# A decoder kernel's first attention: one power for two norms, a second transposed tile, no loop, and the causal mask added by VectorE

## The chip, the cores and the metric

The kernel runs on one core of a Trainium2 chip. The metric is the device time of one execution in microseconds. A core has TensorE (PE), VectorE (DVE), ScalarE (ACT), GpSimd (POOL) and SyncE (SP, which issues the DMAs here). Each works through its own queue in order; semaphores order them against one another. PSUM has 8 banks; one holds 512 float32 per partition.

## The reference

A two-layer decoder on x of 16 batches x 128 tokens x 256 features. The change lies in layer 0's self attention, which in short is:

```
h  = layernorm(x)                      # plain; it is added back below
hn = layernorm(h) * ln_g + ln_b        # a second norm on the first
q, k, v = hn @ wq.T + bq, hn @ wk.T + bk, hn @ wv.T + bv   # 16 heads x 128
q, k = rope(q), rope(k)
p  = softmax(q @ k.T / sqrt(128) + causal)                 # per head, 128 x 128
x  = x + h + (p @ v) @ wo.T + bo
```

This is the first 590 us of the kernel. Retention, a spline layer, window attention, cross attention and a mixture of experts follow, and the change leaves their work as it is.

## The kernel before, in words

`phase_attn0` takes four batches at a time (a group, NG = 4 groups) and in each group one head per step (16 steps), 64 steps in all. Every product that matters is made of three (`matmul3`): operands are kept as a rounded high part and a low rest, in float32r. `step(s, r, g)` is written for each engine: s is the step, r the head, g the group. Step s projects q, k and (in r 0 to 13) one or two pieces of v for head s, works the softmax of head s-2 and the output product of head s-3. `run` writes group 0 out, loops over groups 1 and 2 with a hardware loop (`Fori`), and writes group 3 and three draining steps out.

The order on each engine in a step:

- PE (L604): `project(s)`, with `project_v` behind q and k; a `transpose_x` of the next group's batch in r 5, 7, 9, 11; `out_project(s-3)`; `transpose_p(s-2)`; `score(s-1)`, which first multiplies the bf16 mask with a bf16 identity into the bank SC (L589) and then adds q k^T on top (L592); `weigh(s-2)` (L601).
- DVE (L475): the row maximum of SC for s-2 (L479), `oT_lo` (L482), the reciprocal and P times it (L488), `rope` of q and k (two products each, L455 and L456), then what the step has besides: in group 0 the split of a weight item (L411, r 0 to 12), `add_h` (which adds the norm h to X, L442 and L444), statistics. In r 3, `add_out` (L464) stands before the ropes and `add_const` (L469, L473) behind them.
- ACT (L357): four exponentials with row sums (L363), `sin_q`, a V evacuation, `sin_k` (L372, L380), PT (L386), oT_hi (L390), in group 0 the rounding of weight items.
- POOL: the addition of the two rope products (L322), and the powers to -1/2 (L316, L334).

The high and low parts of the transposed input lie in one pair of tiles, `xT_hi` and `xT_lo`. The next group's are made in r 15: ACT rounds (L355), DVE splits (L448) between the rope of q and the rope of k, and the projection of the next group's head 0 waits for that.

Weights come through two staging buffers (`stage`), in the order of `ITEMS`; an item is loaded, rounded by ACT and split by DVE. The retention phase's inputs are later loaded into the same memory.

Before the first step: statistics of group 0, a power for the first norm, three small DVE operations, a second power, then for each batch in turn normalise (L437), transpose (L539) and evacuate (L348), through one buffer and one bank.

## Time and profile before

| | us |
|---|---|
| median of three runs | 1178.92 (1178.39 to 1179.3) |
| the profiled execution | 1178.37 |
| its span, first to last instruction | 1176.3 |

| engine | busy us | share of the span |
|---|---|---|
| PE | 1023.7 | 87% |
| DVE | 793.6 | 67% |
| ACT | 715.3 | 61% |
| POOL | 315.8 | 27% |

The shares are means over phases with different limits. Starts are counted from the first instruction. A matmul's end is modelled and lies behind the start of the next, so that TensorE is best read by the distance between starts. "idle before <- X" tells how long an engine had stood still and whose result it then had.

### The profile page before, as it was taken

What the parts mean: (1) busy time and instruction counts of PE and PEld (TensorE: products, weight loads), DVE (VectorE), ACT (ScalarE), POOL (GpSimd) and SP (SyncE); (2) the same over time, 40 slices, a digit from 0 to 9 for tenths busy, and PEclk for the clock granted to TensorE, in tenths of its full rate; (3) what the DMA queues carried; (4) which work ended last, traced back from release to release, by engine and by line L of the source; (5) the groups of instructions that cost most, each with busy time, mean ns of one, the idle gap of its engine ahead of it and who ended that gap; (6) DMA issues with size and microseconds to landing.
All of it is one profiled execution on the core that took longest, in us unless ns stands there. A gap on an engine that the chain in (4) does not pass through costs nothing. (4 is left out here: it accounts for less than half of the span.)

```text
span 1176.3 us, 19320 instructions
## 1 busy us (share of the span) xinstructions
PE 1023.7 (87%) x6729; PEld 841.8 (72%) x6757; DVE 793.6 (67%) x1461; ACT 715.3 (61%) x1974; POOL 315.8 (27%) x244
## 2 busy tenths in 40 slices
PE   2789899999899999999878867289999599598997
PEld 2677788888788988898777656267776499474555
DVE  3888876777677766766656777767777534365774
ACT  3577776677667776667533364177777244456883
POOL 1343332323223332232300020134444200101442
PEclk9999999999999999999989878599999799799999
DMA  6111110000000000000070000000000000005342
GB/s 180 55 54 54 37 32 1 1 1 1 2 1 1 1 1 1 1 1 1 1 202 1 1 1 1 1 1 1 2 1 2 1 1 1 14 1 140 102 108 72
DMA packets 31978, 31.80 MB, mean 27 GB/s; under 512 B 8336, under 2 KB 23440, under 8 KB 31888
## 3 DMA queue, kind: packets, MB, share of 16 engines
q1 hardware_dynamic: 31888, 30.60, 9.3%
q8 instruction: 57, 0.93, 0.3%
q14 instruction: 33, 0.27, 0.1%
HBM read 28.36 MB, written 2.23 MB: 26 GB/s over the span
## 5 line engine op out<-in xcount | busy, mean ns | idle before, releaser
L322 POOL TENSOR_TENSOR roped_q<-roped_q,sin_q 128x512 f32<-128x512 f32 x64 | 81.9, 1279 | 323.5 <-DVE sin_q L456 323.5
L35 PE MATMUL banks<-xT_lo,WH 128*128 128x512 f32 x256 | 107.4, 420 | 8.4 <-issue 5.9
L1501 ACT ACTIVATE win_P<-banks,win_neg_max 128x128 f32<-128x128 f32 x256 | 91.1, 382 | 31.2 <-DVE win_neg_max L1567 30.9
L322 POOL TENSOR_TENSOR roped_k<-roped_k,sin_k 128x512 f32<-128x512 f32 x64 | 95.8, 1497 | 52.3 <-DVE sin_k L456 52.3
L363 ACT ACTIVATE P<-banks,neg_max 128x128 f32<-128x128 f32 x256 | 90.3, 370 | 30.8 <-DVE neg_max L479 30.8
L36 PE MATMUL banks<-xT_hi,WL 128*128 128x512 f32 x256 | 102.0, 398 | 0.0
L37 PE MATMUL banks<-xT_hi,WH 128*128 128x512 f32 x256 | 101.9, 398 | 0.0
L390 ACT ACTIVATE oT_hi<-banks,bv_col 128x512 fp32r<-128x512 f32 x64 | 44.1, 688 | 87.6 <-PE banks L601 87.6
L1460 POOL TENSOR_TENSOR win_P<-win_P,win_inv 128x512 f32<-128x512 f32 x64 | 66.6, 1040 | 100.5 <-DVE win_inv L1572 100.3
L372 ACT ACTIVATE sin_k<-banks 64x512 f32<-64x512 f32 x128 | 75.8, 592 | 10.1 <-PE banks L37 8.5
L372 ACT ACTIVATE sin_q<-banks 64x512 f32<-64x512 f32 x128 | 75.8, 592 | 7.7 <-PE banks L37 5.5
L601 PE MATMUL banks<-PT,V 128*128 128x128 f32 x512 | 70.0, 280 | 11.8 <-ACT PT L386 11.8
L582 PE MATMUL banks<-WO_lo,oT_hi 128*128 128x256 f32 x256 | 74.6, 291 | 4.7 <-DVE oT_lo L482 4.7
L601 PEld LDWEIGHTS banks<-PT,V 128*128 128x128 f32 x512 | 62.8, 193 | 15.4 <-ACT PT L386 15.4
L582 PE MATMUL banks<-WO_hi,oT_lo 128*128 128x256 f32 x256 | 72.6, 284 | 0.0
L582 PE MATMUL banks<-WO_hi,oT_hi 128*128 128x256 f32 x256 | 72.3, 282 | 0.0
L592 PEld LDWEIGHTS banks<-roped_k,roped_q 128*128 128x128 f32 x512 | 68.1, 194 | 2.4
L455 DVE SCALAR_TENSOR_TENSOR roped_k<-banks,qk_bias,cos 128x512 f32<-128x512 f32 x64 | 48.0, 750 | 30.9 <-ACT sin_k L372 30.9
L592 PE MATMUL banks<-roped_k,roped_q 128*128 128x128 f32 x512 | 68.3, 277 | 0.0
L2123 POOL TENSOR_TENSOR moe_acc<-moe_acc,moe_weighted 128x512 f32<-128x512 f32 x30 | 38.6, 1289 | 105.6 <-DVE moe_weighted L2241 105.6
L482 DVE SCALAR_TENSOR_TENSOR oT_lo<-banks,bv_col,oT_hi 128x512 fp32r<-128x512 f32 x64 | 47.7, 746 | 28.5 <-ACT oT_hi L390 27.9
L455 DVE SCALAR_TENSOR_TENSOR roped_q<-banks,qk_bias,cos 128x512 f32<-128x512 f32 x64 | 48.0, 750 | 23.9 <-ACT sin_q L372 23.9
(359 smaller groups left out, 3045.1 us busy)
## 6 DMA issues: line engine op xcount, KB each, us to landing
moe_gate_of<-moe_gate_rows SPq DMA_DIRECT2D x32, 256.0 KB, 4.0
X<-in_x SPq DMA_DIRECT2D x4, 512.0 KB, 7.0
stage<-in_wqT SPq DMA_DIRECT2D x4, 512.0 KB, 3.8
stage<-in_wkT SPq DMA_DIRECT2D x4, 512.0 KB, 3.7
stage<-in_wvT SPq DMA_DIRECT2D x4, 512.0 KB, 6.4
stage<-in_woT SPq DMA_DIRECT2D x4, 512.0 KB, 3.8
ctx<-in_ctxT SPq DMA_DIRECT2D x4, 512.0 KB, 6.5
out<-X SPq DMA_DIRECT2D x8, 256.0 KB, 2.8
```

The lines of the kernel that those rows point to most:

```text
L35: nc.tensor.matmul(out, lh, rl, start=first, stop=False)
L36: nc.tensor.matmul(out, ll, rh, start=False, stop=False)
L37: return nc.tensor.matmul(out, lh, rh, start=False, stop=last)
L322: nc.gpsimd.tensor_tensor(roped[w][:, p, :], roped[w][:, p, :], sin_part[w][:], ALU.add).then_inc(roped_sum[w], 1)
L363: ins = nc.scalar.activation(P[:, i, :], SC[:, i * 128:(i + 1) * 128], ACT.Exp, bias=neg_max[:, r % 2, i:i + 1], accum_out=exp_sum[:, r % ...
L372: ins = nc.scalar.activation(sin_part[w][64 * half:64 * half + 64, :], QK[w][64 * (1 - half):64 * (2 - half), :], ACT.Copy)
L455: nc.vector.scalar_tensor_tensor(per_batch(roped[w][:, p, :]), per_batch(QK[w][:]), qk_bias[:, w, r:r + 1], table(cos), ALU.add, ALU.mult) ...
L582: ins = nc.tensor.matmul(OUT[i // 2][:, i % 2 * D:(i % 2 + 1) * D], lhs[:, i, :], rhs[:, ur, :], start=False, stop=True, skip_group_check= ...
L592: ins = nc.tensor.matmul(SC[:, i * 128:(i + 1) * 128], roped[0][:, p, toks], roped[1][:, p, toks], start=False, stop=True, skip_group_chec ...
L601: ins = nc.tensor.matmul(PO[:, i * 128:(i + 1) * 128], V[:, ur // 4 % 2, i, h * 128:(h + 1) * 128], PT[:, i, :], start=True, stop=True)
L1460: nc.gpsimd.tensor_tensor(some, some, inv[:, h % 2, 4 * s:4 * s + 4].rearrange("p (h n) -> p h n", n=1).broadcast_to([128, 4, 128]), ALU.m ...
L1501: ins = nc.scalar.activation(P[:, h % 2, s, i, :], SC[2 * (h % 2) + s][:, i * 128:(i + 1) * 128], ACT.Exp, bias=neg_max[:, h % 2, at:at + ...
```

## The change

1. **One power.** DVE works out the variance of both norms together: with v the variance, `var12 = v * (1 + eps) + eps^2` ahead of one power gives the factor of both (`rstd12`); a second power gives the first norm's own (`rstd`), which only `add_h` needs. `second_norm` and its operations go.
2. **The start.** The first group's four batches are normalised into V's second half, transposed into two banks, and evacuated by two activations; rounding and splitting go by halves. A third staging buffer (over P and PT) holds the third weight item; the order of the first items becomes q, v, k; a projection waits only for its own item.
3. **A tile for odd groups.** `xT_of` is `xT_even` (whose memory the retention inputs take later, as `ret_in`) and `xT_odd` (over the staging buffers). The next group's halves are made in r 13 (ACT) and at the end of r 14 (DVE).
4. **No loop.** All 67 steps are written out, on POOL too.
5. **The mask.** The float32 mask stays as it is loaded. DVE adds it to SC in place, then takes the maximum; the bf16 product, `ident_b` and the bf16 mask go.
6. **Moves.** `add_h` of a group's four batches goes to r 12 to 15 of that group (before: r 0 to 3 for group 0, and r 5, 7, 9, 11 of the group ahead for the others). `add_out` goes from before the ropes of r 3 to the end of r 2. In group 0 the other groups' statistics go from r 0 to 2 to r 4 to 6, the norms to r 7, the normalises to r 8 to 11. The final statistics of groups 0 to 2 go from r 12 to r 8 of group 3.

```diff
-stage = sb("stage", [128, 2, KD, QW])
+with ExitStack() as first:
+    xT_even = sb("xT_even", [128, 2, KD, QW], F32R, first)
+ret_in = sb("ret_in", [128, 2, KD, QW])
...
 cos = sb("cos", [128, 2, S])
 sin = sb("sin", [128, 2, S])
-mask_f = h_of[:, 0:128]
 zeros_b = sb("zeros_b", [128, 128], BF16)
 gb = sb("gb", [128, 2, KD])
 bv_col = sb("bv_col", [128, HEADS0])
-xT_lo = sb("xT_lo", [128, KD, GW], F32R)
+with ExitStack() as first:
+    stage = sb_("stage", [128, STAGES, KD, QW], F32, first)
 sin_part = [sb("sin_q", [128, GW]), sb("sin_k", [128, GW])]
 V = sb("V", [128, 2, GROUP, QW])
+with ExitStack() as first:
...
-ITEMS = [(0, 0), (0, 1), (0, 2)] + [item for q in range(1, QUADS) for item in ((q, 2), (q - 1, 3), (q, 0), (q, 1))] + [(QUADS - 1, 3)]
+ITEMS = [(0, 0), (0, 2), (0, 1)] + [item for q in range(1, QUADS) for item in ((q, 2), (q - 1, 3), (q, 0), (q, 1))] + [(QUADS - 1, 3)]
+def staging(i):
+    if i == STAGES:
+        return stage_P[:], stage_loaded[STAGES], 16
...
-LN_PARTS = ((slice(0, GROUP), GROUP), (slice(GROUP, B), B + 11))
+LN_PARTS = ((slice(0, GROUP), GROUP), (slice(GROUP, B), B + 8))
...
 def run(eng, step):
-        step((NG - 1) * HEADS0 + r, r, NG - 1)
-    for r in range(3):
-        step(STEPS + r, r, NG)
+    for s in range(STEPS + 3):
+        step(s, s % HEADS0, s // HEADS0)
+prepared_at = lambda g: (8, 9, 10, 11) if g == 0 else (4, 6, 8, 10)
+PREPARED = 13
 with nc.Block() as block:
...
-            wait(sp, weights_split, i - STAGES + 1)
+            if i > STAGES:
+                sp.wait_ge(weights_split, i - STAGES if i < 5 else i - 1)
             if w == 3:
                 src = woT[:, 4 * q:4 * q + 4, :]
             else:
                 src = w_src[w][:, :, q * QW:(q + 1) * QW]
-            sp.dma_start(parts(i)[0], src).then_inc(stage_loaded[i % STAGES], 16)
...
-        for i in range(STAGES):
+        for i in range(STAGES + 1):
             load_weights(i)
-        for dst, src in ((mask_f, a["causal"]),
...
-        sp.wait_ge(weights_split, len(ITEMS))
-        held = stage[:].rearrange("p s k n -> p (s k n)")
+        sp.wait_ge(projected[1], (NG - 1) * HEADS0)
+        sp.wait_ge(v_projected, (NG - 1) * HEADS0)
...
+        def powers(part):
             some, n = LN_PARTS[part]
-            pool.wait_ge(ln0, n + 7 + 3 * second)
-            nc.gpsimd.tensor_tensor((rstd, rstd2)[second][:, some], var_eps[:, some], minus_half[:, some], ALU.pow).then_inc(rstd_ready, 1)
+            pool.wait_ge(ln0, n + 8)
+            nc.gpsimd.tensor_tensor(rstd12[:, some], var12[:, some], minus_half[:, some], ALU.pow).then_inc(rstd_ready, 1)
+            nc.gpsimd.tensor_tensor(rstd[:, some], var_eps[:, some], minus_half[:, some], ALU.pow).then_inc(rstd_ready, 1)
         def step(t, p):
...
+        for t in range(STEPS):
             step(t, t % 2)
-            if t in (2, 3):
-                power(1, t - 2)
-        with pool.Fori(2, STEPS // 2) as i:
-            for p in range(2):
-                step(i * 2 + p, p)
-        pool.wait_ge(ln0, B + 29)
+            if t == 7:
+                powers(1)
...
+            wait(act, xT_split, KD * group)
             for k in range(KD):
             ins.then_inc(xT_evacuated, 1)
+        def first_xT():
+            act.wait_ge(x_transposed, GROUP)
+            for k in range(KD):
+                nc.scalar.activation(xT_full[:, k, :], bank[3 + k], ACT.Identity, bias=gb[:, 1, k:k + 1], scale=gb[:, 0, k:k + 1]).then_inc(xT_evacuated, GROUP // KD)
+            for k in range(KD):
+                act.wait_ge(xT_evacuated, GROUP // KD * (k + 1))
+                nc.scalar.activation(xT_even[:, 0, k, :], xT_full[:, k, :], ACT.Copy).then_inc(xT_rounded, 1)
         def round_xT(g):
             act.wait_ge(xT_evacuated, GROUP * g + GROUP)
-            wait(act, projected[1], HEADS0 * g)
-            nc.scalar.activation(xT_hi[:], xT_full[:], ACT.Copy).then_inc(xT_rounded, 1)
+            if g == 1:
+                act.wait_ge(weights_split, len(ITEMS))
+            wait(act, projected[1], HEADS0 * (g - 1))
...
                 act.wait_ge(max_found, 1 + u)
+                if u == 0:
+                    act.wait_ge(weights_split, STAGES + 1)
...
-            if r == 15 and live(g + 1, NG):
+            if r == PREPARED and g + 1 < NG:
                 round_xT(g + 1)
...
-        for i in range(STAGES):
-            round_weights(i)
+            if g + 1 < NG and r - 1 in prepared_at(g):
+                i = prepared_at(g).index(r - 1)
+                evacuate_xT((g + 1) * GROUP + i, i, g + 1)
+        round_weights(0)
         act.wait_ge(first_loaded, 48)
-        for b in range(GROUP):
-            evacuate_xT(b, b, 0)
-        round_xT(0)
+        first_xT()
+        round_weights(1)
         round_weights(2)
...
+            nc.vector.tensor_scalar(var12[:, some], ln_tmp[:, 4, some], (1.0 + LN_EPS) / D, LN_EPS * LN_EPS, ALU.mult, ALU.add).then_inc(ln0, 1)
...
-            wait(dve, x_transposed, b)
-            nc.vector.tensor_scalar(xn[:], batch(X, b), one(mean, b), one(rstd12, b), ALU.subtract, ALU.mult).then_inc(xn_ready, 1)
+            dve.wait_ge(rstd_ready, 1 if b < GROUP else 3)
+            if b >= GROUP:
+                dve.wait_ge(x_transposed, b)
+            dst = V[:, 1, b, 0:D] if b < GROUP else xn[:]
+            nc.vector.tensor_scalar(dst, batch(X, b), one(mean, b), one(rstd12, b), ALU.subtract, ALU.mult).then_inc(xn_ready, 1)
...
+            dve.wait_ge(rstd_ready, 2 if b < GROUP else 4)
...
-            dve.wait_ge(xT_rounded, g + 1)
-            nc.vector.tensor_tensor(xT_lo[:], xT_full[:], xT_hi[:].bitcast(F32), ALU.subtract).then_inc(xT_split, 1)
+            for k in (range(KD) if g == 0 else (slice(0, KD),)):
+                dve.wait_ge(xT_rounded, k + 1 if g == 0 else KD * g + KD)
+                nc.vector.tensor_tensor(xT_of[g % 2][:, 1, k], xT_full[:, k], xT_of[g % 2][:, 0, k].bitcast(F32), ALU.subtract).then_inc(xT_split, 1 if g == 0 else KD)
...
                 dve.wait_ge(scored, u + 1)
+                nc.vector.tensor_tensor(SC.rearrange("p (h n) -> p h n", h=GROUP), SC.rearrange("p (h n) -> p h n", h=GROUP), four(mask[:]), ALU.add).then_inc(masked, 1)
+                dve.wait_ge(masked, u + 1)
                 nc.vector.tensor_reduce(neg_max[:, r % 2, :], SC[:].rearrange("p (h n) -> p h n", h=GROUP), AX.X, ALU.max, negate=True).then_inc(max_found, 1)
...
-                if r == 3 and live(g - 1, NG):
-                    add_out(g - 1)
                 rope(s, r % 2, r, 0)
-                if r == 15 and live(g + 1, NG):
-                    split_xT(g + 1)
                 rope(s, r % 2, r, 1)
-            if isinstance(g, int) and g == 0:
+            if g == 0:
                 for i in split_at(r):
                     split_weights(i)
-                if r < GROUP:
-                    add_h(r)
-                if r < 3:
-                    group_stats(r + 1)
-                if r in (2, 3, 4):
-                    (first_stats, second_stats, both_norms)[r - 2](1)
-            if r == 3 and live(g - 1, NG):
+                if r in (4, 5, 6):
+                    group_stats(r - 3)
+                if r == 7:
+                    both_norms(1)
+            if r == 2 and 0 < g < NG:
+                add_out(g - 1)
+            if r == 3 and 0 < g < NG:
                 add_const(g - 1)
-            if r == 12 and isinstance(g, int) and g == NG - 1:
+            if r == 8 and g == NG - 1:
                 dve.wait_ge(restated, NEXT)
-                finish_stats(nc, dve, ln0, B + 22, stats[:, 0:NEXT, :], mean[:, 0:NEXT], var_eps[:, 0:NEXT], ln_tmp[:, :, 0:NEXT], LN_EPS)
-            if r in (4, 6, 8, 10) and live(g + 1, NG):
-                normalise(g * GROUP + GROUP + (r - 4) // 2)
-            if r in (5, 7, 9, 11) and live(g + 1, NG):
-                add_h(g * GROUP + GROUP + (r - 5) // 2)
+                finish_stats(nc, dve, ln0, B + 16, stats[:, 0:NEXT, :], mean[:, 0:NEXT], var_eps[:, 0:NEXT], ln_tmp[:, :, 0:NEXT], LN_EPS)
+            if g + 1 < NG and r in prepared_at(g):
+                normalise((g + 1) * GROUP + prepared_at(g).index(r))
+            if g + 1 < NG and r == PREPARED + 1:
+                split_xT(g + 1)
+            if g < NG and r >= HEADS0 - GROUP:
+                add_h(g * GROUP + r - (HEADS0 - GROUP))
...
-        first_stats(0)
-        split_weights(0)
-        second_stats(0)
-        split_weights(1)
         both_norms(0)
+        dve.wait_ge(ln0, GROUP + 8)
         for b in range(GROUP):
             normalise(b)
+        split_weights(0)
+        split_xT(0)
+        split_weights(1)
+        split_weights(2)
         dve.wait_ge(consts_loaded, 16 * 11)
-        nc.vector.tensor_copy(ident_b[:], ident[:]).then_inc(consts_made, 1)
-        nc.vector.tensor_copy(mask[:], mask_f).then_inc(consts_made, 1)
         nc.vector.memset(zeros_b[:], 0.0).then_inc(consts_made, 1)
-        split_xT(0)
-        split_weights(2)
...
-            wait(pe, xT_evacuated, b)
+            if b >= GROUP:
+                pe.wait_ge(xT_evacuated, b)
             for k in range(KD):
-                ins = nc.tensor.transpose(XB[:, k * 128:(k + 1) * 128], xn[:, k * 128:(k + 1) * 128], ident[:])
+                dst, src = (bank[3 + k][:, b * S:(b + 1) * S], V[:, 1, b, :]) if b < GROUP else (XB[:, k * 128:(k + 1) * 128], xn)
+                ins = nc.tensor.transpose(dst, src[:, k * 128:(k + 1) * 128], ident[:])
...
-                pe.wait_ge(xT_split, g + 1)
-            if isinstance(g, int) and g == 0 and r % 4 == 0:
-                pe.wait_ge(weights_split, split_by[r // 4, 1])
+                pe.wait_ge(xT_split, KD * (g + 1))
             cols = slice(r * DK0, (r + 1) * DK0)
+            xT_hi, xT_lo = xT_of[g % 2][:, 0], xT_of[g % 2][:, 1]
             for w in range(2):
+                if g == 0 and r % 4 == 0:
+                    pe.wait_ge(weights_split, split_by[r // 4, w])
...
-            nc.tensor.matmul(SC[:], ident_b[:], four(mask[:]), start=True, stop=True)
+            if u == 0:
+                pe.wait_ge(consts_made, 1)
             for i in range(GROUP):
                 toks = slice(i * S, (i + 1) * S)
-                ins = nc.tensor.matmul(SC[:, i * 128:(i + 1) * 128], roped[0][:, p, toks], roped[1][:, p, toks], start=False, stop=True, skip_group_check=True)
+                ins = nc.tensor.matmul(SC[:, i * 128:(i + 1) * 128], roped[0][:, p, toks], roped[1][:, p, toks], start=True, stop=True)
...
-            if r in (5, 7, 9, 11) and live(g + 1, NG):
-                transpose_x(g * GROUP + GROUP + (r - 5) // 2)
+            if g + 1 < NG and r - 1 in prepared_at(g):
+                transpose_x((g + 1) * GROUP + prepared_at(g).index(r - 1))
```

## Rows read from the trace of the kernel before

**Rows 1.** Windows: stretch, length, busy us and instructions per engine, granted clock, DMA share, GB/s.

```profile
170.00:310.00 140.00, 134.92 (x839) 118.81 (x840) 100.70 (x156) 96.54 (x258) 43.41 (x33) 0.99 0.00 1
```

**Rows 2.** Timeline, TensorE: start, duration, engine, line, operation. Scores of steps 17, 28, 33, 44, 49, 60.

```profile
189.61 1.05 PE L592 MATMUL banks<-roped_k,roped_q 128*128 128x128 f32 x8
...
281.27 1.05 PE L592 MATMUL banks<-roped_k,roped_q 128*128 128x128 f32 x8
...
326.58 1.05 PE L592 MATMUL banks<-roped_k,roped_q 128*128 128x128 f32 x8
...
418.25 1.05 PE L592 MATMUL banks<-roped_k,roped_q 128*128 128x128 f32 x8
...
460.61 1.05 PE L592 MATMUL banks<-roped_k,roped_q 128*128 128x128 f32 x8
...
551.28 1.05 PE L592 MATMUL banks<-roped_k,roped_q 128*128 128x128 f32 x8
```

**Rows 3.** Timeline, VectorE: the maximum in steps 2, 7, 8, 9, 13, 14, 16, 63, 64.

```profile
44.44 0.68 DVE L479 TENSOR_REDUCE neg_max<-banks 128x4 f32<-128x512 f32 x1
...
94.89 0.68 DVE L479 TENSOR_REDUCE neg_max<-banks 128x4 f32<-128x512 f32 x1
...
104.48 0.68 DVE L479 TENSOR_REDUCE neg_max<-banks 128x4 f32<-128x512 f32 x1
...
113.62 0.68 DVE L479 TENSOR_REDUCE neg_max<-banks 128x4 f32<-128x512 f32 x1
...
149.79 0.68 DVE L479 TENSOR_REDUCE neg_max<-banks 128x4 f32<-128x512 f32 x1
...
156.50 0.68 DVE L479 TENSOR_REDUCE neg_max<-banks 128x4 f32<-128x512 f32 x1
...
172.30 0.68 DVE L479 TENSOR_REDUCE neg_max<-banks 128x4 f32<-128x512 f32 x1
...
567.89 0.68 DVE L479 TENSOR_REDUCE neg_max<-banks 128x4 f32<-128x512 f32 x1
...
574.60 0.68 DVE L479 TENSOR_REDUCE neg_max<-banks 128x4 f32<-128x512 f32 x1
```

**Rows 4.** Timeline, VectorE: sin product of k in step 63, beside GpSimd's addition.

```profile
573.35 1.32 DVE L456 SCALAR_TENSOR_TENSOR sin_k<-sin_k,rot_bias,sin 128x512 f32<-128x512 f32 x1
```

**Rows 5.** Timeline, VectorE and GpSimd: second half of an add_h, and the addition beside it.

```profile
225.21 1.38 DVE L444 TENSOR_TENSOR X<-X,h_of 128x256 f32 x1
...
224.92 1.37 POOL L322 TENSOR_TENSOR roped_k<-roped_k,sin_k 128x512 f32<-128x512 f32 x1 [0.78 <-DVE sin_k L456]
```

**Rows 6.** Timeline: mask product and scores of a step, its maximum, the first exponential.

```profile
526.91 0.38 PE L589 MATMUL banks<-mask,ident_b 128*128 128x512 bf16 x1
...
527.13 1.05 PE L592 MATMUL banks<-roped_k,roped_q 128*128 128x128 f32 x8
...
528.22 0.69 DVE L479 TENSOR_REDUCE neg_max<-banks 128x4 f32<-128x512 f32 x1 [0.32 <-PE banks L592]
...
529.70 0.36 ACT L363 ACTIVATE P<-banks,neg_max 128x128 f32<-128x128 f32 x1
```

**Rows 7.** Groups by line, to 590 us: shapes, count, busy us, mean ns, idle before.

```profile
L464 DVE TENSOR_TENSOR X<-banks,X 128x512 f32 x4 | 2.6, 683 | 0.0
...
L455 DVE SCALAR_TENSOR_TENSOR roped_k<-banks,qk_bias,cos 128x512 f32<-128x512 f32 x64 | 48.0, 750 | 30.9 <-ACT sin_k L372 30.9
```

**Rows 8.** Timeline: first power, first normalise, first projection product.

```profile
7.38 1.02 POOL L316 TENSOR_TENSOR rstd<-var_eps,minus_half 128x4 f32<-128x4 f32 x1 [6.54 <-DVE var_eps L61]
...
13.97 0.41 DVE L437 TENSOR_SCALAR xn<-X,mean,rstd 128x256 f32<-128x256 f32 x1
...
23.49 0.77 PE L35 MATMUL banks<-xT_lo,WH 128*128 128x512 f32 x1 [3.29 <-issue]
```

**Rows 9.** Windows: 3 us behind TensorE's wait at the loop's second pass; its first product.

```profile
307.50:310.50 3.00, 2.64 (x6) 2.15 (x7) 1.12 (x3) 1.21 (x8) 0.34 (x1) 0.52 0.02 5
...
307.86 0.79 PE L35 MATMUL banks<-xT_lo,WH 128*128 128x512 f32 x1 [2.56 <-issue]
```

More of the change, by code:

```diff
@@ L182, in phase_attn0 @@
         consts_loaded = sem("consts_loaded")
-        stage_loaded = [sem(f"stage{i}_loaded") for i in range(STAGES)]
+        stage_loaded = [sem(f"stage{i}_loaded") for i in range(STAGES + 1)]
         weights_rounded = sem("weights_rounded")
@@ L345, in evacuate_xT @@
                     act.wait_ge(x_transposed, b + 1)
-                    wait(act, xT_split, group)
+                    wait(act, xT_split, KD * group)
                     for k in range(KD):
@@ L2430, in weights_ahead, with phase_rest @@
     return w, transfers
-def phase_rest(nc, a, sem, sb, banks, bank, X, ident, mean, var_eps, rstd, minus_half, stats, ln_tmp, out, clear_semaphores, free_attn0, stage, out_bias, ret_loaded):
+def phase_rest(nc, a, sem, sb, banks, bank, X, ident, mean, var_eps, rstd, minus_half, stats, ln_tmp, out, clear_semaphores, free_attn0, ret_in, out_bias, ret_loaded):
     t = (nc, a, sem, sb, bank, X, ident, mean, var_eps, rstd, minus_half, stats, ln_tmp)
```

65 lines of the change are left out of this document (26 added, 39 removed).

## The prediction

> **What bounds the kernel now.** First I read busy time by stretch. Between 170 and 310 us TensorE is busy 96% of the time, VectorE 72%, ScalarE 69%, the granted clock at 0.99 [rows 1]. So the first attention (to about 590 us) is mostly TensorE's, and everything behind 590 us is untouched by the diff. Then I read when the scores of successive steps begin (one step is one head of one group of four batches; I count steps 0 to 63, and by "score n" I mean the start of step n's score products) and when VectorE's maximum begins [rows 2, 3]. Score 49 to score 60 takes 90.67 us for eleven steps, mostly 8.05 each. But in group 0 the maxima are 9.59 and 9.14 apart, and there TensorE waits.
>
> A second circle turns there, which I call the **round**: maximum (0.6), four exponentials (1.5), sin_q (1.2), V (0.6) and sin_k (1.2) in order on ScalarE, k's rope on VectorE (1.4), VectorE's extra work of the step, then the next maximum. Bare, it takes 6.71 (149.79 to 156.50). In a step without V it takes 6.71 as well (567.89 to 574.60): V's evacuation falls away, but the sin product of k then runs beside GpSimd and takes 1.32 [rows 3, 4]. In group 0 the weight split with a normalise makes 9.14, with an add_h 9.59. An add_h alone, beside GpSimd's addition of 1.37, holds VectorE 1.74 us (its second half alone is 1.38) [rows 5]. Whatever makes a round longer than TensorE's step of 8.05 (6.65 without V) sets the pace as soon as the slack of some 2 us is used.
>
> **The change, part by part.**
>
> *The mask.* TensorE loses the bf16 product: 526.91 to the score at 527.13 is 0.22 us in each of 64 steps [rows 6]. VectorE gains a 128x512 add in place in PSUM. No row shows VectorE writing PSUM. The nearest is the add of a bank and X, 0.683; the rope product that reads a bank and a table takes 0.750 [rows 7]. I bound it by 0.55 and 0.85 (with its wait) and take 0.69 and 0.04 for the handoff to the maximum, 0.73 in all, as it is nearest to the first. Where TensorE paces, the add is covered: today the maximum starts at 528.22, 1.09 after the score at 527.13, but ScalarE comes to the exponentials only at 529.70, 2.57 after it, because oT_hi is in front of them [rows 6]; mask and maximum end at 1.09 + 0.73 + 0.65 = 2.47. There the step gains 0.22. Where the round paces, the step loses 0.73. A covered add would thus be worth 14 us of TensorE time over 64 steps, an uncovered one costs 47.
>
> The rope product with one operand in a bank keeps 0.75 with GpSimd running, that with both in SBUF takes 1.32 [rows 4, 7]. The Trainium skill (GPSIMD Engine Reference, 1. Specifications) says VectorE and GpSimd collide when VectorE has two SBUF inputs or uses a 2-port mode; by it the mask add, with one SBUF input, isn't lengthened but add_h is, and the trace agrees. The same skill (VectorE: DVE Perf Modes, Rules for kernel authors) tells authors to minimise the number of chained operations, semaphores being free; that speaks against a second pass over the scores. By its table (The TRN2 errata) a 512-element pass with a PSUM source is 120 + 512 cycles at 0.96 GHz, 0.66 us, an estimate by which the total would be 1 us lower.
>
> *The start.* Today the first projection begins at 23.49 [rows 8]. Afterwards one power instead of two stands before the normalise. GpSimd starts the first at 7.38 and takes 1.02; the second follows at once and holds off the first normalise until about 9.4. Four normalises (0.41 each, the last part of one under the start of the next) end at 10.8 [rows 8]. The four batches go to two banks without waiting for one another, so the transposes are in at 11.5. ScalarE then takes two 128x512 evacuations and two roundings of 0.6 (to 13.9), VectorE two splits of 0.65, the second behind the last rounding (to 14.7). First projection 14.9: **-8.6**. The third weight's transfer now stands before the constants in the queue; it is 512 KB and is needed only at about 17, the constants too.
>
> *Projection to first maximum.* Today 44.44 - 23.49 = 20.95 [rows 3, 8]. VectorE's two add_h (1.8 each) and two sets of statistics (1.3 each) leave the queue ahead of it, 6.2; a little of that was covered by waits: **-5.6**.
>
> *Group 0, first maximum to that of step 13.* Today 149.79 - 44.44 = 105.35 [rows 3]. All of it is rounds, so all pay 0.73. Steps 2 and 3 (split only): 7.84 + 0.73 = 8.57 each; steps 4 to 6 with statistics 9.9 each; step 7 with the small ones of the norms 10.0; steps 8 to 11 9.14 + 0.73 = 9.87 each; step 12 with split and add_h 9.59 + 0.73 = 10.32. Sum 106.65: **+1.3**. The two powers between steps 7 and 8 hold GpSimd 4.6 us, done before the next rope.
>
> *Group 0, steps 13 to 16.* Rounds: 13: 6.71 + 0.73 + 1.74 = 9.18; 14, with the split of xT and add_h: 6.71 + 0.73 + 2.88 = 10.32; 15: 9.18. Sum 28.7 against 172.30 - 149.79 = 22.51 [rows 3]: **+6.2**. From there to score 17, 17.31 today [rows 2, 3], the mask comes once, the product goes: **+0.3**.
>
> *Middles.* Score 17 to 28 is 91.66 today, 49 to 60 90.67 [rows 2]. Eleven times 0.22 is -2.4; constants and statistics stay at step 3, where the mask makes a late round later still: +1.2. **-1.2** in groups 1 and 2, **-0.3** in group 3, where the final statistics move to step 8. Moving add_out ahead of step 3 relieves TensorE of 0.3; counted in.
>
> *Boundaries.* Score 28 to 33 is 45.31, score 44 to 49 42.36 [rows 2]. The difference, 2.95, is the loop's branch: TensorE is idle 2.56 us before 307.86, and the granted clock falls to 0.52 over the next 3 us, which is the lower level, 1.2 GHz [rows 9]. Afterwards nothing branches, and the double xT lets projections go on. But all four add_h now stand in steps 12 to 15, two of which have no V and need TensorE only 6.43. In rounds from score 27: mask 1.45 behind it, step 12 9.6 (ScalarE evacuates xT before the exponentials), then 9.18, 10.32, 9.18, and 17.4 to score 33: 57.1, less 7.8 to score 28: 49.3. **+4.0** and **+6.9**. Before, each add_h of these groups stood in a step with 8.05 us of TensorE's work and was hidden.
>
> *End.* Group 3 had no add_h; now it has four. From score 60 to the maximum of step 64 it was 574.60 - 551.28 = 23.32 [rows 2, 3]; now 2.6 + 3 x 9.18 = 30.1, **+6.8**, and **+0.3** in the tail, where the mask is partly beside oT_hi.
>
> Sum: -8.6 - 5.6 + 1.3 + 6.2 + 0.3 - 1.2 - 1.2 - 0.3 + 4.0 + 6.9 + 7.1 = +8.9. At each boundary TensorE will wait 2 to 3 us at once, which as at the branch can halve the clock for its next products [rows 9]. Three times about 0.5, mostly inside waits: +1.5. The profiled execution took 1178.37 us around a span of 1176.3, 0.55 below the median of 1178.92. 1178.37 + 10.4 = 1188.8; against the median 1189.
>
> **The rivals.**
> *TensorE stays the bound* (the faster side). If slack between the queues takes up the late add_h, boundaries fall to TensorE's own work: 0 instead of +6.2, -4.1 and -1.1 instead of +4.0 and +6.9, -0.7 at the end. Sum -21: 1158. For it speaks TensorE's 96% [rows 1]; against it group 0, where rounds of 9.59 pace steps worth 8.05 [rows 3]. It decides at a round of 6.43 + 2 in step 14; I forecast 10.3. 12%.
> *add_h is short* when it misses GpSimd: 0.75 instead of 1.74, 16 times with 1 us each but partly slack: about 1176. For it: the first halves are 0.4. Against: GpSimd starts its addition 0.13 behind the product each time [rows 5]. 8%.
> *The start gains nothing*, the change not doing what it says, as the third weight or the constants land late: +5 at most, 1194. 8%.
> *The mask in PSUM is dear*, 0.85 or more, or each stall also halves the clock: some 30 round-paced steps at 0.12 and more, and 1.7 per drop: 1196 to 1204. 12%.
> *The forecast* 60%, 1182 to 1195, by the mask's two bounds.
>
> **How the numbers follow.** The range 1174 to 1200 leaves out the first rival and the dearest part of the fourth, about 17%. A measurement can tell about 0.2%, 2.4 us, from no change. Faster: both first rivals, 0.20. Same: the edges between, 0.06. Slower 0.74.
>
> **What the profile would show.** First projection near 15 us; the mask add at 0.69 and maxima 0.73 behind it; score to score 7.83 in group 3's middle; 10.3 between maxima of steps 14 and 15, with TensorE waiting for P and PT there; score 44 to 49 near 49; the end of the first attention about 10 us later than 587. I am wrong if TensorE shows no waits in steps 13 to 16, or if add_h takes under 1 us.

## The result: 1.3% slower, and where the time went

The changed kernel takes 1194.04 us (median of 4, 1193.29 to 1197.06), the kernel before 1178.66 (1177.82 to 1179.3): a ratio of 1.0134, 95% interval 1.0115 to 1.0152. The profiled execution took 1193.29 us around a span of 1191.5, so the two traces are 15.2 us apart in span. Among the executions of the experiments below two took far longer, one of the kernel before (1877 us) and one with the mask product back (3451 us), and the ratios leave them out. The forecast was 1189, slower, with a range of 1174 to 1200.

From the page of the kernel after (busy us, share and instructions):

```profile
PE 1020.9 (86%) x6665; PEld 836.6 (70%) x6693; DVE 836.6 (70%) x1518; ACT 717.5 (60%) x1969; POOL 318.6 (27%) x244
```

VectorE has 43 us more to do than before (793.6), TensorE 3 less (1023.7). That alone doesn't say what is lost. The scores of steps 17, 28, 33, 44, 49 and 60 after, in the timeline of TensorE (start, duration, engine, line, operation), answer to [rows 2]:

```profile
184.59 1.06 PE L602 MATMUL banks<-roped_k,roped_q 128*128 128x128 f32 x8
...
275.52 1.06 PE L602 MATMUL banks<-roped_k,roped_q 128*128 128x128 f32 x8
...
326.52 1.06 PE L602 MATMUL banks<-roped_k,roped_q 128*128 128x128 f32 x8
...
416.74 1.06 PE L602 MATMUL banks<-roped_k,roped_q 128*128 128x128 f32 x8
...
466.31 1.06 PE L602 MATMUL banks<-roped_k,roped_q 128*128 128x128 f32 x8
...
557.19 1.06 PE L602 MATMUL banks<-roped_k,roped_q 128*128 128x128 f32 x8
```

At score 17 the changed kernel is 5.02 us ahead (189.61 before); it loses that and more at the two boundaries and at the end. By the stages of the forecast, in us, changes of length:

| stage | before | after | change | forecast |
|---|---|---|---|---|
| to the first projection | 23.49 | 14.63 | -8.9 | -8.6 |
| to the first maximum | 20.95 | 17.06 | -3.9 | -5.6 |
| group 0, to the maximum of step 13 | 105.35 | 107.34 | +2.0 | +1.3 |
| to the maximum of step 16 | 22.51 | 28.72 | +6.2 | +6.2 |
| to score 17 | 17.31 | 16.84 | -0.5 | +0.3 |
| middle, scores 17 to 28 | 91.66 | 90.93 | -0.7 | -1.2 |
| boundary, 28 to 33 | 45.31 | 51.00 | +5.7 | +4.0 |
| middle, 33 to 44 | 91.67 | 90.22 | -1.4 | -1.2 |
| boundary, 44 to 49 | 42.36 | 49.57 | +7.2 | +6.9 |
| middle, 49 to 60 | 90.67 | 90.88 | +0.2 | -0.3 |
| score 60 to the end of the attention | 36.30 | 44.96 | +8.7 | +7.1 |
| everything behind it | 588.72 | 589.35 | +0.6 | 0 |

The last row is work that the change leaves alone. In the kernels below it lies between 588.1 and 592.5, with the places where the clock is lowered, so that a single trace of a span says nothing under some 4 us; the stages in front of it repeat much more closely (below, two kernels agree in them within 0.04).

What such a stretch looks like in the changed kernel, here in group 0, steps 14 and 15: VectorE's timeline (same columns; split of xT, add_h, mask, maximum; then add_h, mask, maximum), with ScalarE's first exponential between the two. In brackets stands the idle time ahead of an instruction, and whose result it then had:

```profile
154.94 1.21 DVE L458 TENSOR_TENSOR xT_odd<-xT_full,xT_odd 128x1024 fp32r<-128x1024 f32 x1
156.07 1.38 DVE L451 TENSOR_SCALAR h_of<-X,mean,rstd 128x256 f32<-128x256 f32 x1
157.48 0.42 DVE L453 TENSOR_TENSOR X<-X,h_of 128x256 f32<-128x256 f32 x1
157.82 0.69 DVE L489 TENSOR_TENSOR banks<-banks,mask 128x512 f32<-128x512 f32 x1
158.55 0.69 DVE L491 TENSOR_REDUCE neg_max<-banks 128x4 f32<-128x512 f32 x1
...
159.28 0.37 ACT L379 ACTIVATE P<-banks,neg_max 128x128 f32<-128x128 f32 x1 [3.38 <-DVE neg_max L491]
...
165.27 0.40 DVE L451 TENSOR_SCALAR h_of<-X,mean,rstd 128x256 f32<-128x256 f32 x1
165.70 1.40 DVE L453 TENSOR_TENSOR X<-X,h_of 128x256 f32<-128x256 f32 x1
167.03 0.69 DVE L489 TENSOR_TENSOR banks<-banks,mask 128x512 f32<-128x512 f32 x1
167.75 0.69 DVE L491 TENSOR_REDUCE neg_max<-banks 128x4 f32<-128x512 f32 x1
```

On VectorE split, add_h, mask and maximum follow one another with no idle time, and ScalarE waits for the maximum, 3.38 us here. Between the two maxima lie 9.20 us (the forecast had 9.18), in the step before, with the split, 10.34 (10.32); before, the round of step 13 took 6.71 [rows 3].

And TensorE waits for it. From its timeline at the first boundary:

```profile
300.36 0.39 PE L591 MATMUL banks<-WO_lo,oT_hi 128*128 128x256 f32 x1 [2.43 <-DVE oT_lo L494]
...
304.30 1.16 PE L611 MATMUL banks<-PT,V 128*128 128x128 f32 x8 [0.57 <-ACT PT L402]
...
312.27 0.50 PE L35 MATMUL banks<-WL,xT_even 128*128 128x512 f32 x1 [2.71 <-ACT V L396]
...
313.61 0.63 PE L37 MATMUL banks<-WH,xT_even 128*128 128x512 f32 x1
...
317.16 1.06 PE L602 MATMUL banks<-roped_k,roped_q 128*128 128x128 f32 x8
```

V's evacuation (L396) frees the bank that the second product of V for head 0 needs; it stands behind sin_q in ScalarE's queue, so behind the late maximum of 308.14. TensorE had run ahead into the next group and stood still there for 2.71 us. Some 1.1 us later its clock is halved (the row of 313.61: 0.63 where such a product takes 0.39). The same two places at the second boundary:

```profile
453.58 0.50 PE L35 MATMUL banks<-WL,xT_odd 128*128 128x512 f32 x1 [2.02 <-ACT V L396]
...
456.93 1.06 PE L602 MATMUL banks<-roped_k,roped_q 128*128 128x128 f32 x8
```

The wait for V is there as well, and it ends at the same place: 36.75 us behind score 28 at the first boundary, 36.84 behind score 44 at the second. The next score comes at 41.64 and at 40.19. So the 1.4 us by which the first boundary is the longer lie behind the wait, where the first has the lowered clock and the second 1.00. The window with the lowered clock (length; busy us and instructions of PE, PEld, DVE, ACT, POOL; granted clock, DMA share, GB/s):

```profile
313.40:316.80 3.40, 3.40 (x16) 3.20 (x15) 1.47 (x2) 0.64 (x2) 2.28 (x2) 0.50 0.00 0
```

0.50 is the lower level, 1.2 GHz, for 3.4 us in which TensorE is busy throughout, on the path to score 32.

### The profile page after: what moved, and what is told of

Its sections match the earlier page's. It is cut to its first block and busy times, and to the rows that moved or that the text cites. A ratio compares the mean times of both kernels' runs of the same rounds, so it can differ in the third digit from the quotient of the medians.

```text
span 1191.5 us, 18922 instructions
## 1 busy us (share of the span) xinstructions
PE 1020.9 (86%) x6665; PEld 836.6 (70%) x6693; DVE 836.6 (70%) x1518; ACT 717.5 (60%) x1969; POOL 318.6 (27%) x244
## 5 line engine op out<-in xcount | busy, mean ns | idle before, releaser
L329 POOL TENSOR_TENSOR roped_k<-roped_k,sin_k 128x512 f32<-128x512 f32 x64 | 99.5, 1555 | 43.8 <-DVE sin_k L466 43.8
L611 PE MATMUL banks<-PT,V 128*128 128x128 f32 x512 | 73.4, 287 | 26.3 <-ACT PT L402 26.1
L591 PEld LDWEIGHTS banks<-WO_lo,oT_hi 128*128 128x128 f32 x256 | 49.1, 192 | 29.0 <-DVE oT_lo L494 23.8
L602 PEld LDWEIGHTS banks<-roped_k,roped_q 128*128 128x128 f32 x512 | 63.5, 195 | 0.1
L2236 DVE TENSOR_TENSOR moe_hidden<-banks,moe_squared 128x512 f32<-128x512 f32 x64 | 44.1, 689 | 27.0 <-PE banks L2343 18.0
L1576 DVE TENSOR_REDUCE win_neg_max<-banks 128x8 f32<-128x1024 f32 x32 | 39.2, 1224 | 28.2 <-PE banks L1705 28.2
L35 PE MATMUL banks<-xT_even,WH 128*128 128x512 f32 x128 | 53.8, 420 | 3.5 <-DVE xT_even L458 3.5
```

Of the source, the lines that this page charges most:

```text
L35: nc.tensor.matmul(out, lh, rl, start=first, stop=False)
L329: nc.gpsimd.tensor_tensor(roped[w][:, p, :], roped[w][:, p, :], sin_part[w][:], ALU.add).then_inc(roped_sum[w], 1)
L591: ins = nc.tensor.matmul(OUT[i // 2][:, i % 2 * D:(i % 2 + 1) * D], lhs[:, i, :], rhs[:, ur, :], start=False, stop=True, skip_group_check= ...
L602: ins = nc.tensor.matmul(SC[:, i * 128:(i + 1) * 128], roped[0][:, p, toks], roped[1][:, p, toks], start=True, stop=True)
L611: ins = nc.tensor.matmul(PO[:, i * 128:(i + 1) * 128], V[:, ur // 4 % 2, i, h * 128:(h + 1) * 128], PT[:, i, :], start=True, stop=True)
L2236: TT(dst, U1[s % 3], squared[:, s % 2, :], ALU.mult).then_inc(hidden_done, 1)
```

## The experiments

The theory to be tested: what counts is the round (maximum, exponentials, sin_q, V, sin_k, k's rope, VectorE's extras). The mask costs each round-paced step 0.73, and add_h costs 1.8 in each because it stands where no wait covers it. The rivals: TensorE's own slack, the clock, or the written-out loop are behind the loss.

### add_h back in the middle: where it hurts depends on the mask

For groups 1 to 3, `add_h` goes from r 12 to 15 to r 5, 7, 9, 11 of its own group.

```diff
-if g < NG and r >= HEADS0 - GROUP:
+if g == 0 and r >= HEADS0 - GROUP:
     add_h(g * GROUP + r - (HEADS0 - GROUP))
+if 0 < g < NG and r in (5, 7, 9, 11):
+    add_h(g * GROUP + (r - 5) // 2)
```

> The changed kernel with the add_h of groups 1 to 3 moved from steps 12 to 15 of a group to its steps 5, 7, 9 and 11; group 0 and all else as changed. Theory of the round (mask 0.73 and add_h 1.74 both lengthen the circle through VectorE and ScalarE): a middle step with add_h now has a round of 7.44 + 1.74 = 9.18 against TensorE's 7.88, so what the boundaries give back is mostly lost in the middles: about 1191 us, 3 less than changed. Rival (the place at the boundary is the cause, since two of those steps have no V): the boundaries of groups 1 to 2, 2 to 3 and the end lose their +5.7, +7.2 and +8.7 us and nothing comes in their place: about 1173 us.

Measured: 1188.26 us, ratio to before 1.0074 (1.0046 to 1.0101), span 1185.9. Scores 28 to 33 now take 44.11, 44 to 49 44.27, the end 39.77: 6.9, 5.3 and 5.2 less. But the middles take 93.83, 93.60 and 94.58: 2.9, 3.4 and 3.7 more. In the kernel before the same place was free: there, with an add_h or a normalise of the same steps in front of it, the maximum begins 1.5 to 2.2 behind the scores, and ScalarE comes to the exponentials 2.6 to 3.3 behind them anyway, because oT_hi and in some steps an evacuation of xT are in front. Here, with the mask add as well, the maximum begins 3.6 to 3.7 behind the scores, and ScalarE waits for it. Scores, mask, maximum and first exponential of one step of this run:

```profile
219.70 1.06 PE L604 MATMUL banks<-roped_k,roped_q 128*128 128x128 f32 x8
...
222.69 0.69 DVE L489 TENSOR_TENSOR banks<-banks,mask 128x512 f32<-128x512 f32 x1
...
223.41 0.69 DVE L491 TENSOR_REDUCE neg_max<-banks 128x4 f32<-128x512 f32 x1
...
224.14 0.37 ACT L379 ACTIVATE P<-banks,neg_max 128x128 f32<-128x128 f32 x1 [1.01 <-DVE neg_max L491]
```

Two additions that would each be covered share one cover, and together they exceed it. Of the 17.4 us that boundaries and end give back, the middles take 10.0, and the first attention gains 7.4. So the rival, by which nothing comes in their place (1173), is refuted, and the late add_h's place at the boundary is only one part of its price.

### The mask back on TensorE

The mask product, its bf16 tiles and their two conversions return; all else is as in the changed kernel.

```diff
-nc.vector.tensor_tensor(SC.rearrange("p (h n) -> p h n", h=GROUP), SC.rearrange("p (h n) -> p h n", h=GROUP), four(mask[:]), ALU.add).then_inc(masked, 1)
-dve.wait_ge(masked, u + 1)
...
+nc.tensor.matmul(SC[:], ident_b[:], four(mask[:]), start=True, stop=True)
...
```

> The changed kernel with the mask again as a bf16 product on TensorE, VectorE's add taken out. Theory of the round: 0.73 less in each of some 30 steps that the round paces, 0.22 more in those that TensorE paces: bare rounds back to 6.7, steps 8.05 in the middles, about 1176 us, 18 less than changed. Rival (the add is covered, and only the late add_h costs): TensorE's 0.22 comes back in about 40 steps and nothing else: about 1200 us, slower than changed.

Measured: 1175.36 us, 0.9954 (0.9937 to 0.9972), span 1173.7: 17.8 less than the changed kernel. The part from the first maximum to that of step 13, eleven rounds, falls by 7.36 (0.67 each), the boundaries by 2.7 and 2.8, the end by 3.0. The middles fall by 0.2, 0.1 and 0.9 though TensorE has the product to do again. Steps 13 to 16 of group 0 fall by 1.8, but the stretch from there to score 17 rises by 1.9 (18.76 against 16.84): in this trace the clock is lowered from 161.8 to 165.2 (0.53), and in the kernel with both edits below, where it isn't, that stretch takes 17.19. So as placed the add gains nothing where TensorE paces and loses where the round does.

### The mask add on the kernel before

First the loop alone: the kernel before with its 67 steps written out (its only edits are in `run` and in POOL's loop).

```diff
-with eng.Fori(1, NG - 1) as g:
-    for r in range(HEADS0):
-        step(g * HEADS0 + r, r, g)
...
+for s in range(STEPS + 3):
+    step(s, s % HEADS0, s // HEADS0)
```

> The kernel before with its loops written out, on all engines, and nothing else. If the branch's cost of 2.95 us between groups 1 and 2 (45.31 against 42.36 us from score 28 to 33 and 44 to 49) is the branch's alone: a span 2.9 us shorter, 1173.4. Rival: the rounds at that boundary (xT's rounding and split in step 15) are nearly as late as the branch, and only part comes back: 1 us or less.

Measured: 1176.07 us, 0.9969 (0.9957 to 0.9981), span 1177.1. Scores 28 to 33 go from 45.31 to 42.37, exactly the length of the second boundary (42.37), and the first attention as a whole is 3.0 shorter. The wait of 2.56 for the branch is gone, and so is the lowered clock behind it, where [rows 9] had 0.52. Windows and the first wait of TensorE there:

```profile
307.50:310.50 3.00, 2.32 (x10) 1.52 (x9) 1.74 (x4) 2.94 (x11) 0.50 (x1) 1.00 0.00 0
...
310.66 0.50 PE L35 MATMUL banks<-WL,xT_hi 128*128 128x512 f32 x1 [0.84 <-ACT V L370]
```

In its profiled run the work behind the attention, which is unchanged, takes 3.8 us more, so that the span itself (1177.1) doesn't show the gain; the timed runs give 0.3% faster, 3.2 us.

Then the same with the float32 mask added by VectorE, as in the change:

> The same, with the mask added by VectorE in place instead of the product; order, start and add_h as before. Theory of the round: group 0 pays 0.73 in 11 rounds (8 us), the middles, with an add_h of 1.74 in every second step, reach 9.2 + 7.8 against twice 7.9 and pay 1 to 2 us in each pair, the boundary with xT's split in step 15 and the end pay too: about 1193 to 1198, some 20 more than without the add. Rival (TensorE is busy 96% and paces, the add is covered): 14 us less than without it, 1160.

Measured: 1195.67 us, 1.0146 (1.0118 to 1.0173), span 1193.0. The first attention is 19.9 us longer than in the kernel with the loop written out: 8.05 in the eleven rounds up to step 13, where 11 x 0.73 = 8.03; 1.7 to the maximum of step 16; 2.2 in each of the first two middles (here the mask meets the add_h of steps 5, 7, 9 and 11, as in the first experiment); 1.9 and 2.0 at the boundaries; 2.4 at the end; only the third middle, which has no add_h, gains, by 0.7 (its steps fall from 8.06 to 7.90). The mask add is a loss by itself, with none of the other edits beside it.

### add_h in VectorE's waits

`add_h` is cut in two. h itself (L451) is worked out behind oT_lo, while ScalarE works the exponentials; the addition to X (L455) behind P, while ScalarE works sin_q. The steps stay r 12 to 15, the mask stays with VectorE.

```diff
+def add_h2(b):
     dve.wait_ge(h_added, 2 * b + 1)
     nc.vector.tensor_tensor(batch(X, b), batch(X, b), h_of[:], ALU.add).then_inc(h_added, 1)
...
                        ALU.add, ALU.subtract).then_inc(oT_lo_ready, 1)
+    if g < NG and r >= HEADS0 - GROUP:
+        add_h(g * GROUP + r - (HEADS0 - GROUP))
     if live(u, STEPS):
         dve.wait_ge(exps_done, u + 1)
...
+    if g < NG and r >= HEADS0 - GROUP:
+        add_h2(g * GROUP + r - (HEADS0 - GROUP))
     if live(s, STEPS):
         rope(s, r % 2, r, 0)
...
-    if g < NG and r >= HEADS0 - GROUP:
-        add_h(g * GROUP + r - (HEADS0 - GROUP))
```

> The changed kernel with each add_h, still in steps 12 to 15, cut in two and put where VectorE waits for ScalarE inside the round: its first half behind oT_lo (VectorE waits 0.9 us for the exponentials there), its second behind P times 1/sum (it waits 0.3 us for sin_q). Same instructions, mask on VectorE. Theory of the round: add_h costs the round nothing, rounds of steps 12 to 15 fall from 9.2 and 10.3 to 7.4 and 8.6, about 1168 us, 26 less than changed. Rival (VectorE's total load in those steps decides, or GpSimd's sharing): no change, 1194 us, or a few us worse as P comes later.

Measured: 1165.4 us, 0.9876 (0.9848 to 0.9904), span 1163.7: 27.8 less than the changed kernel. Steps 13 to 16 of group 0 fall from 28.72 to 23.99, the boundaries from 51.00 and 49.57 to 42.98 and 43.06, the end from 44.96 to 38.71, and the step before 13 by 1.8. The groups of VectorE by shape, up to the end of the attention (count, busy us, mean ns, idle before), first of the changed kernel:

```profile
L489 DVE TENSOR_TENSOR banks<-banks,mask 128x512 f32<-128x512 f32 x64 | 44.0, 688 | 14.8 <-PE banks L602 14.5
L453 DVE TENSOR_TENSOR X<-X,h_of 128x256 f32<-128x256 f32 x16 | 18.4, 1150 | 0.6
L451 DVE TENSOR_SCALAR h_of<-X,mean,rstd 128x256 f32<-128x256 f32 x16 | 10.3, 646 | 0.0
```

then with add_h in the waits:

```profile
L455 DVE TENSOR_TENSOR X<-X,h_of 128x256 f32<-128x256 f32 x16 | 6.7, 418 | 0.0
L451 DVE TENSOR_SCALAR h_of<-X,mean,rstd 128x256 f32<-128x256 f32 x16 | 6.5, 404 | 0.0
```

28.7 us of VectorE's time become 13.2, since GpSimd is at rest at both places, and the 13.2 that are left lie under waits. The Trainium skill (GPSIMD Engine Reference, 1. Specifications) has the two engines collide where VectorE has two SBUF inputs or uses a 2-port mode. The trace agrees for the X + h add (0.42 against 1.40) and for the mask add with its one SBUF input (0.69 wherever it stands, about half of them beside a GpSimd operation). The first half of add_h, with one SBUF tensor, is held too (0.40 against 1.38).

Whether anything of add_h is still paid was asked by leaving it out:

> The changed kernel with no add_h at all: h is not added to x, so this part of the computation is left out. If add_h in VectorE's waits (the run that came to 1165 us) really costs nothing, this is within 1 us of it in its span, 1163.7. Rival: the operations in the waits still cost something (two SBUF inputs beside GpSimd, P's product delayed): 3 us or more below it.

Measured: 1168.03 us, 0.9908 (0.9886 to 0.993), span 1164.9. Without it every stage from the first maximum to the end of the attention is within 0.04 us of the kernel that does it in the waits (42.98 at both first boundaries, 38.69 against 38.71 at the end), but for a start 0.2 later. In the waits, sixteen add_h cost nothing that these stages show. (The timed runs, of two sets, have the kernel without add_h 2.6 us slower; the intervals of the two ratios overlap.)

### Both, and the mask by step

> Both together: mask as a product and add_h in VectorE's waits, on top of the rest of the change. Theory of the round: no round of groups 1 to 3 exceeds TensorE's step but the one with constants and statistics; 1152 to 1156 us, and the two effects do not add up to 18 + 26 = 44 since they shorten the same rounds. Rival (two independent causes): 1194 - 44 = 1150 us or less.

Measured: 1152.37 us, 0.9763 (0.9737 to 0.9789), span 1149.9. The two edits took 17.8 and 27.8 from the changed kernel's span, together 41.6; from its first attention 18.4 and 27.5, together 43.3. The two causes nearly add, which the forecast had doubted; its 1152 to 1156 holds all the same. The boundaries are 41.79 and 41.73 now, the end 36.28: near the 41.2 and 41.3 that the first rival worked out for a boundary paced by TensorE alone.

The mask can also be added by VectorE only where it is covered, for heads 3 to 12 of groups 1 to 3 (30 of 64), here from the bf16 tile, and be a product elsewhere. This starts from the kernel with both edits:

```diff
+added = lambda u: u >= HEADS0 and 3 <= u % HEADS0 <= 12
...
+if not added(u):
     nc.tensor.matmul(SC[:], ident_b[:], four(mask[:]), start=True, stop=True)
```

> add_h in VectorE's waits, and the mask by place: added by VectorE (from a bf16 tile) for heads 3 to 12 of groups 1 to 3, where steps have one V and TensorE paces, and a product for all of group 0 and the other heads. Theory of the round: against the run with the product throughout (1152.4 us, span 1149.9) the middles gain 0.16 in each of about 27 steps, nothing is lost: 1148 us, span about 1146. Rival (any pass more on VectorE costs): slower than 1152.

Measured: 1145.89 us, 0.9711 (0.9687 to 0.9734), span 1146.0. The middles fall from 90.75, 90.11 and 89.97 to 89.47, 88.79 and 89.44. That is 3.1 us, at 0.1 and 0.2 more in the boundaries (the timed runs, of two sets, differ by 6.5). A step with the product (the kernel with the mask back on TensorE) and one with the add (this one), timeline:

```profile
380.69 0.38 PE L602 MATMUL banks<-mask,ident_b 128*128 128x512 bf16 x1
...
382.00 0.69 DVE L491 TENSOR_REDUCE neg_max<-banks 128x4 f32<-128x512 f32 x1 [0.53 <-PE banks L605]
...
384.16 0.37 ACT L381 ACTIVATE P<-banks,neg_max 128x128 f32<-128x128 f32 x1
```

```profile
381.60 0.68 DVE L495 TENSOR_TENSOR banks<-banks,mask 128x512 f32<-128x512 f32 x1
...
382.32 0.69 DVE L497 TENSOR_REDUCE neg_max<-banks 128x4 f32<-128x512 f32 x1
...
383.66 0.37 ACT L382 ACTIVATE P<-banks,neg_max 128x128 f32<-128x128 f32 x1
```

In the first the maximum ends at 382.69 and ScalarE comes 1.5 later; in the second it ends at 383.01 and ScalarE still comes 0.65 later. The add is hidden, and a step that TensorE paces falls from 8.03 to 7.88, by 0.15 and not by the 0.22 that the forecast gave the product. Not every step is such a one: the step with the final statistics in group 3 rises from 8.04 to 8.68, so the third middle gains least (0.5).

### The norms in the waits as well

The statistics (now in r 3 to 5) and the normalises of the groups to come go behind oT_lo too, the norms to r 6, GpSimd's powers go one step earlier, and the transposes and the evacuation of xT follow in the step of their normalise, not one later.

```diff
                        ALU.add, ALU.subtract).then_inc(oT_lo_ready, 1)
+    if g == 0 and r in (3, 4, 5):
+        group_stats(r - 2)
+    if g + 1 < NG and r in prepared_at(g):
+        normalise((g + 1) * GROUP + prepared_at(g).index(r))
...
-        if r in (4, 5, 6):
-            group_stats(r - 3)
...
-    if g + 1 < NG and r in prepared_at(g):
-        normalise((g + 1) * GROUP + prepared_at(g).index(r))
```

> e8_mask_by_step, with the other work of VectorE in a step (the statistics of groups 1 to 3 and the normalise of a later tile) moved from in front of the maximum or behind the exps' wait to the place behind oT_lo, where VectorE waits for ScalarE. My theory, that a VectorE instruction lengthens a round only where no wait covers it, expects steps 3 to 5 and 8 to 11 of group 0 to fall from about 9.2 to about 8.3 us a round, other groups by less because TensorE bounds them: some 6 us less than e8_mask_by_step, 1140 us. Rival: the statistics and the normalise are longer than the wait (0.4 to 0.7 us of it is left beside add_h), hold up the next product of VectorE or the transposes of TensorE, and nothing or less than nothing is gained: 1146 us or more.

Measured: 1142.1 us, 0.9691 (0.9675 to 0.9707), span 1138.2. The stage from the first maximum to that of step 13 falls from 98.19 to 93.03; the others stay within 0.2. VectorE's timeline with statistics, first as it was (step 4: the split of a weight, statistics, maximum), then in the wait (step 5):

```profile
53.19 1.21 DVE L429 TENSOR_TENSOR WL<-stage,WH 128x1024 fp32r<-128x1024 f32 x1
54.33 1.39 DVE L434 BATCH_NORM_STATS2 stats<-X 128x6 f32<-128x256 f32 x4
55.64 0.67 DVE L497 TENSOR_REDUCE neg_max<-banks 128x4 f32<-128x512 f32 x1
```

```profile
55.01 0.73 DVE L500 SCALAR_TENSOR_TENSOR oT_lo<-banks,bv_col,oT_hi 128x512 fp32r<-128x512 f32 x1
55.67 1.39 DVE L434 BATCH_NORM_STATS2 stats<-X 128x6 f32<-128x256 f32 x4
56.98 0.15 DVE L510 RECIPROCAL inv_sum<-exp_sum 128x4 f32<-128x4 f32 x1
```

The statistics fill the wait to the brim (no idle time is shown before the reciprocal). The round of step 4 falls from 9.69 to 8.40 and that of step 5 from 9.15 to 7.98. Steps 6 and 7 together fall by 1.15, though the small operations of the norms now lengthen step 6 (10.11). The gain is 0.8 short of the 6 expected, and it is the normalises that fall short: the rounds of steps 8 to 12 fall by only 1.6 in all. Step 8 falls from 9.15 to 7.97, but steps 9 to 11 only to 8.88, 8.68 and 8.68, and step 12, ahead of whose exponentials the last evacuation stands, rises from 7.84 to 8.67. VectorE's share of a normalise is covered (0.40 each where they had been 1.39), but ScalarE's is not:

```profile
97.19 0.68 DVE L497 TENSOR_REDUCE neg_max<-banks 128x4 f32<-128x512 f32 x1
...
98.05 0.80 ACT L354 ACTIVATE xT_full<-banks,gb 128x128 f32<-128x128 f32 x2
...
98.73 0.38 ACT L382 ACTIVATE P<-banks,neg_max 128x128 f32<-128x128 f32 x1
```

The first exponential now begins 1.54 behind the maximum's start instead of 0.71, because oT_hi, the rounding of a weight and the evacuation of xT are in front of it on ScalarE, and the maximum comes too early to cover them. With VectorE's extras gone ScalarE's are next on the round. This is the fastest kernel here, 3.1% below the one before and 4.3% below the change (1142.1 against 1194.04; that last comparison is across two sets of runs).

## Why the prediction was right, and which terms were off

The sign and the mechanism held; the span rose by 15.2 us where 10.4 were forecast (8.9 of steps, 1.5 of clock).

**What bounds what.** The forecast let the round pace group 0, the boundaries and the end, and TensorE the middles. It had for rounds 8.57, 9.87 to 9.9, 10.32, 9.18, 10.32, 9.18; the trace has 8.56, 9.87 to 9.89, 10.34, 9.18, 10.34, 9.20. The one round that is off is that of step 7 (below). The experiments bear it out with both causes taken away in turn. At steps 13 to 16 TensorE waits, as forecast, but longest for oT_lo (2.43 at 300.36) and for V's bank, where the forecast named P and PT.

**The mask.** 0.69 with 0.04 of handoff, taken between bounds of 0.55 and 0.85 from the nearest rows [rows 7], measured 0.688 and 0.03 to 0.04. Eleven rounds with it cost 8.05.

**The start.** -8.6 was -8.9, and GpSimd's first power begins at 7.52, 0.14 later than before [rows 8]; its second no longer holds off the first normalise.

```profile
7.52 1.02 POOL L322 TENSOR_TENSOR rstd<-var,minus_half 128x4 f32<-128x4 f32 x1 [6.67 <-DVE var L438]
8.51 1.01 POOL L323 TENSOR_TENSOR rstd<-var_eps,minus_half 128x4 f32<-128x4 f32 x1
8.66 1.38 DVE L445 TENSOR_SCALAR V<-X,mean,rstd 128x256 f32<-128x256 f32 x4 [1.29 <-POOL rstd L322]
```

**Projection to first maximum.** -5.6 was -3.9, as large a miss as the first boundary's. Two items of the term were wrong. It left out the mask, which stands in front of the first maximum as well (the kernel with the product is 1.5 shorter here; 0.7 is the mask add, and 0.7 is that TensorE's first products stand 0.43 apart until 19.9 us in the change and until 18.2 there, 0.23 afterwards). And of the two add_h that leave, at 1.8 each, the first has no addition of GpSimd beside it: its two halves took 0.82 in the kernel before, as its timeline shows:

```profile
34.88 0.40 DVE L442 TENSOR_SCALAR h_of<-X,mean,rstd 128x256 f32<-128x256 f32 x1
35.32 0.42 DVE L444 TENSOR_TENSOR X<-X,h_of 128x256 f32<-128x256 f32 x1
```

**Group 0.** +1.3 was +2.0. The difference is step 7, 10.7 instead of 10.0: the first of the norms' small operations, on 12 elements, takes 1.27 beside GpSimd's addition and ends with it, and its like right behind it takes 0.17.

```profile
85.33 2.22 POOL L329 TENSOR_TENSOR roped_k<-roped_k,sin_k 128x512 f32<-128x512 f32 x1 [0.63 <-DVE sin_k L466]
...
86.31 1.27 DVE L51 TENSOR_TENSOR ln_tmp<-stats 128x12 f32<-128x12 f32 x1
87.51 0.17 DVE L52 TENSOR_TENSOR ln_tmp<-stats 128x12 f32<-128x12 f32 x1
```

The forecast used GpSimd's hold on wide operations and took the small ones at their bare size. Steps 13 to 16, +6.2, were exact.

**Middles.** -1.2, -1.2, -0.3 were -0.7, -1.4, +0.2. The product's term was too large: a step that TensorE paces falls from 8.05 to 7.88, by 0.17 and not by 0.22 (with the product back it takes 8.03), so score to score is 7.88 in group 3 where 7.83 was forecast. It is right that this is mostly given back at the late rounds of steps 3 and 4, and the second experiment confirms it (with the product back, the first two middles differ by under 0.2). In group 3 the final statistics in step 8 add a second late round, 0.8 between scores 57 and 58, also with a 12-element operation of 1.14 beside GpSimd's addition.

**Boundaries.** +4.0 and +6.9 (49.3 each) were +5.7 and +7.2 (51.00 and 49.57). The branch's part, 2.95, was exact by the written-out loop. Of the rounds only that of step 12 was off (9.97 and 9.80, not 9.6). The stretch from the last mask add to score 33 or 49, taken as 17.4 for both, is 19.1 at the first and 17.6 at the second; the first has the lowered clock in it.

**The clock.** +1.5 was put down for three drops. The trace has four of 3.4 us each, from 146.1, 313.4, 443.1 and 589.9, with the granted clock at 0.51, 0.50, 0.51 and 0.50. The first and the third lie in steps that the round paces, and their rounds are no longer for it (9.18 and 9.20); the second and the last are paid. The second makes the 1.5 by which the first boundary exceeds the other (19.1 against 17.6): the wait ahead of it ends at the same place in both. The last lies in the drain and wasn't priced by itself. So the total of 1.5 was on the low side, and its spread over three equal places wrong: the drop on TensorE's path costs 1.5 alone, not 0.5 (as does the one in the kernel with the product, 18.76 against 17.19), and those that a round covers cost nothing.

**The end.** +7.1 was +8.7. Three rounds of 9.2 were as forecast; the first maximum behind score 60 comes 3.4 after it, not 2.6, since an add_h already stands in front of it; and in the drain the mask costs its whole 0.7 and the scores of the last step run at the lower clock (592.83, 1.30 instead of 1.05).

```profile
592.83 1.30 PE L602 MATMUL banks<-roped_k,roped_q 128*128 128x128 f32 x8
```

**The rivals.** That TensorE's slack would take up the late add_h (1158) is refuted for the change as it stands. The kernel with both causes removed, though (span 1149.9), lands at about that rival's boundaries and under its time. That add_h is short was wrong where the change puts it, and right where GpSimd is at rest. The start gained what it was to. The dear mask did not come.

What stays open: why the work behind the attention differs by up to 4 us between kernels in which it is the same. The places of the lowered clock differ with it, but no run changed one and kept the rest. Nor does any row show what makes the clock fall behind one wait and not behind another that is as long.

## What to carry to other kernels

An operation moved from an engine with 96% of its time taken to one with 72% can still lose where that one sits on a recurrence; compare the length of the round, not the busy shares, and count all the extras of a step against one cover. Small work belongs where its engine waits for another inside the round, in reach of the operand it needs: the same sixteen additions cost about 27 us behind the ropes and nothing behind oT_lo and P. Where an operation has two homes, choose by step: the product where the round paces, the add where TensorE does.
